# Attention stages two and three: score products issued ahead of the transposes, and one-pass float32r products for batches 4 to 7

## The reference, cut to what matters

```python
# first cross attention (stage "at2"): x_context has 77 tokens
q = layernorm((x_query @ Wq).reshape(B, Nq, H, D).transpose(0, 2, 1, 3), ln_g, ln_b) * SCALE
k = layernorm(k, ln_g, ln_b)
attn = jax.nn.softmax(jnp.einsum('bhqd,bhkd->bhqk', q, k), axis=-1)
out = jnp.einsum('bhqk,bhkd->bhqd', attn, v)
return out.transpose(0, 2, 1, 3).reshape(B, Nq, H * D) @ Wp + bp
# second cross attention (stage "at5"): the same with a mask
scores = jnp.einsum('bhqd,bhkd->bhqk', Q, K) / jnp.sqrt(jnp.float32(D_K))
attn_w = jax.nn.softmax(jnp.where(mask, -jnp.inf, scores), axis=-1)
```

## Time and profile before

| | |
|---|---|
| runs of the kernel before | median 405.69 us of 3 (404.98 to 406.9) |
| profiled execution | 410.61 us, span 408.8 us |
| mean granted clock of TensorE in it | 0.976 |
| busy of the span | PE 371.3 us (91%), DVE 285.3 (70%), ACT 223.5 (55%), POOL 142.3 (35%) |
| chain that ended last | PE 77%, DVE 12%, ACT 6%, issue 3% |
| `at2`, first `scores` to last `weigh` | 68.8 to 116.2 us |
| `at5`, first `scores` to last `weigh` | 264.5 to 308.2 us |

### The profile page before, as it was taken

One profiled execution on the slowest core, in us unless ns is written; L12 is line 12 of the kernel. 1 busy time (PEld: TensorE's weight loads), 2 busy tenths in 40 slices (PEclk: granted clock), 3 DMA queues, 4 the chain that ended last, 5 costly groups with the idle time before them and its releaser, 6 DMA issues.

```text
span 408.8 us, 10122 instructions
## 1 busy us (share of the span) xinstructions
PE 371.3 (91%) x4062; PEld 254.5 (62%) x4066; DVE 285.3 (70%) x729; ACT 223.5 (55%) x423; POOL 142.3 (35%) x130
## 2 busy tenths in 40 slices
PE   5989997798998999999999999789998999999990
PEld 2556675666775846566677777456774566666670
DVE  6767878447875785789899786676876544444456
ACT  2855568445568167899999981235454522222210
POOL 6929952571232150027889782100012000000002
PEclk9999999669999999999999999999999999999996
DMA  6420000000000000132232310360000000000001
GB/s 176 87 52 4 4 2 2 2 2 3 2 2 2 0 2 0 22 102 79 84 111 87 106 40 2 110 201 3 4 3 1 2 0 1 2 0 2 0 2 52
DMA packets 16883, 13.86 MB, mean 34 GB/s; under 512 B 6548, under 2 KB 14133, under 8 KB 16837
## 3 DMA queue, kind: packets, MB, share of 16 engines
q1 hardware_dynamic: 15538, 12.51, 10.5%
q10 hardware_dynamic: 1299, 0.71, 0.6%
HBM read 12.64 MB, written 0.57 MB: 32 GB/s over the span
## 4 chain that ended last, share of the span: by engine, by line
PE 77%; DVE 12%; ACT 6%; issue 3%; POOL 1%; POOLq 0%; DVEq 0%
PE PS L2005 10%; PE PS L2093 7%; PE PS L2097 7%; PE PS L2124 7%; PE PS L1581 6%; PE PS L1520 6%; PE PS L1601 5%; PE PS L1992 5%; PE PS L1560 5%; PE PS L1526 3%; PE PS L1650 2%; DVE mxp L1053 2%; PE PS L1515 2%; PE PS L1804 2%; DVE untransposed L1319 2%
## 5 line engine op out<-in xcount | busy, mean ns | idle before, releaser
L663 ACT ACTIVATE att<-PS 77x512 f32<-77x512 f32 (+1 forms) x96 | 51.7, 591 | 44.6 <-PE PS L1584 44.6
L1053 DVE TENSOR_REDUCE mxp<-PS 128x4 f32<-128x308 f32 (+1 forms) x96 | 48.1, 536 | 15.5 <-PE PS L1560 15.4
L910 ACT ACTIVATE kM<-PS 128x512 f32<-128x512 f32 x32 | 19.1, 597 | 55.4 <-PE PS L2093 55.4
L516 POOL TENSOR_TENSOR rstd<-ve,neg_half 128x1 f32<-128x1 f32 x24 | 14.2, 593 | 81.5 <-DVE ve L981 81.5
L510 POOL TENSOR_TENSOR rstd<-ve,neg_half 128x4 f32<-128x4 f32 x6 | 6.2, 1025 | 103.9 <-DVE ve L940 103.9
L1370 DVE TENSOR_TENSOR_SCAN big<-big,PS 128x768 f32<-128x768 f32 x22 | 38.3, 1747 | 5.2 <-PE PS L1992 4.8
L1459 DVE TENSOR_TENSOR big<-kM,PS 128x512 f32<-128x512 f32 x32 | 21.9, 687 | 27.3 <-PE PS L2097 26.0
L2093 PE MATMUL PS<-xT,V 128*128 128x512 f32 x64 | 33.0, 597 | 1.1 <-DVE xT L1447 0.8
L2097 PE MATMUL PS<-xT,V 128*128 128x512 f32 x64 | 32.7, 592 | 0.0
L2124 PEld LDWEIGHTS PS<-big 128*128 128x128 f32 x256 | 29.7, 192 | 3.4 <-issue 3.4
L2124 PE MATMUL PS<-big 128*128 128x128 f32 x256 | 29.7, 275 | 0.0
(11 more groups left out here) (367 smaller groups left out, 870.3 us busy)
## 6 DMA issues: line engine op xcount, KB each, us to landing
kM<-Cdram SPq DMA_DIRECT2D x6, 384.0 KB, 3.4
XH<-Cdram SPq DMA_DIRECT2D x5, 384.0 KB, 3.3
xT<-Cdram SPq DMA_DIRECT2D x5, 384.0 KB, 3.5
V<-in_L_ffn_Wg SPq DMA_DIRECT2D x1, 1024.0 KB, 5.6
V<-in_L_ffn_Wu SPq DMA_DIRECT2D x1, 1024.0 KB, 8.2
out_x<-X SPq DMA_DIRECT2D x2, 256.0 KB, 2.7
ctxN<-in_ctx ACTq DMA_DIRECT2D x1, 308.0 KB
X<-in_x ACTq DMA_DIRECT2D x1, 256.0 KB, 3.8
```

Source lines behind the costliest of these rows:

```text
L663: A_(PT[0:nk, i % 2, g], bank4(at.bank("exp", i, g), nk), ACT.Exp, scale=at.scale)\
L1053: V_.tensor_reduce(mxp[:, b % 3, g, 0:J], PS[:, at.bank("max", b, g), 0:J * nk].rearrange("p (j k) -> p j k", j=J), axis=AX.X, op=ALU.max) ...
```

## The change

Four things change in `at2` and `at5`; `at1` keeps its order.

1. PE issues `scores(i + 2)` ahead of `flips(i)` instead of behind it (with the order of the banks to match). ACT takes all four exponentials of a batch before its copy of `flipped`. DVE takes the four maxima right behind the copy of `outT`, and `residual`, the reciprocal and `normalise` come behind the remainders.
2. For batches 4 to 7 the products of `shifted` use new tiles `K4` and `Q4` in float32r. Each 32-row group now holds one head, 8 rows by 4 combinations of a high and a low part of key and query, so that one product sums high by high, low by high, high by low and low by low.
3. The parts are made by POOL (`split`: a copy that rounds to 12 bits, and a difference), for the late queries of `at2` by a second ACT copy and a DVE difference (`late_low`). SP stores each into a DRAM scratch in 4 transfers (`pack`), and POOL loads them back into `K4` and `Q4` (`unpack`). For `at2` one more ACT copy makes `key2_raw` from bank `k2.1`, behind the first of the four masked copies. For `at5` POOL makes the masked keys of the second half instead of DVE.
4. `keep_busy` gets 2 products ahead of `scores(0)` of `at2`, and 4 ahead of `scores(1)`. The load of the expert weights waits until the last packed part has been loaded.

```diff
+def slots(scores_first):
+    bursts = [("max", 0), ("flip", -1), ("max", 1)]
+    for i in range(B):
+        after = [("flip", i), ("max", i + 2)][::-1 if scores_first else 1]
+        bursts += [("exp", i)] + [(what, n) for what, n in after if n < B]
+    return [(what, i, g) for what, i in bursts for g in range(1 if what == "flip" else G)]
...
+        def pack(dst, high, low, n, order):
+            if n > 2:
+                sp.wait_ge(event(f"packed{n % 2}_stored"), 4 * 16 * ((n - 1) // 2))
+            rows = dst.rearrange("(h c d) n -> c h d n", c=4, d=HD)
+            for c, part in enumerate(order):
+                sp.dma_start(rows[c], high if part == "h" else low, allow_slow_non_contiguous=True)\
+                    .then_inc(event(f"packed{n % 2}_stored"), 16)
...
+        sp.wait_ge(event("split"), KEYS2_SPLIT)
+        pack_keys(k2_packed, key2_high, key2_low, 1)
+        for b in range(HB):
+            sp.wait_ge(at2.late, b + 1)
+            sp.wait_ge(event("late_low"), b + 1)
+            pack_queries(q2_packed[b], XH[:, b, :], XH[:, HB + b, :], 2 + b)
...
+        for b in range(HB):
+            sp.wait_ge(event("split"), QUERIES5_SPLIT[b])
+            pack_queries(q5_packed[b], sq[:, b, :], XH[:, b, :], 7 + b)
         sp.wait_ge(dring.full, dring.index["dl.1"] + 1)
+        sp.wait_ge(event("packed_loaded"), 16 * 10)
         sp.dma_start(Wg6, a["L1_ffn_Wg"].rearrange("e d n -> d e n")).then_inc(experts_loaded, 16)
...
+        def split(x, high, low, done):
+            P_.tensor_copy(high.bitcast(F32R), x).then_inc(event("split"), 1)
+            pool.wait_ge(event("split"), done - 1)
+            P_.tensor_tensor(out=low.bitcast(F32R), in0=x, in1=high, op=ALU.subtract).then_inc(event("split"), 1)
+        def unpack(dst, src, n):
+            pool.wait_ge(event(f"packed{n % 2}_stored"), 4 * 16 * ((n + 1) // 2))
+            if n > 1:
+                pool.wait_ge(event("packed_loaded"), 16 * (n - 1))
+            P_.dma_start(dst, src.rearrange("(g p) n -> p g n", g=G).bitcast(F32R),
+                         allow_slow_non_contiguous=True).then_inc(event("packed_loaded"), 16)
...
                 if 0 <= i < B:
-                    exponentials(i, (0, 1))
+                    exponentials(i, range(G) if at.scores_first else (0, 1))
...
+                if at.scores_first:
+                    if done:
+                        weighted_copy(at, n)
+                    if ahead:
+                        maximum(i + 2, 0)
+                        maximum(i + 2, 1)
...
+                        maximum(i + 2, 2)
+                        maximum(i + 2, 3)
+                        remainder(i + 2, 0)
+                    if left:
+                        apply(at, b)
+                    if ahead:
+                        remainder(i + 2, 1)
+                    if added:
+                        residual(at, r)
+                    if done:
+                        normalise(at, n, inverse(at, n))
+                    if added:
+                        statistics(at, r)
...
+                if at.packs(b):
+                    at.packed.wait_loaded(pe, b)
...
+                        if at.packs(b):
+                            keys, queries = at.packed.keys(g, j, b), at.packed.queries(g, j, b)
...
                 if 0 <= i - 1 < B:
                     weigh(i - 1)
+                if at.scores_first and i + 2 < B:
+                    scores(i + 2)
                 if i < B + 3:
                     flips(i)
...
         def queries_turned(n):
+            keep_busy(at2.bank("max", 0, 1), 2)
...
+        def first_half_scored():
+            pe.wait_ge(at1.residual_ready, B)
+            keep_busy(at2.bank("max", 1, 0), 4)
```

218 lines of the change are left out of this document (146 added, 72 removed).

## The result

The changed kernel takes 413.32 us (median of 4 executions, 410.77 to 415.28), the kernel before 406.26 beside it; the ratio is 1.015, with a 95% interval of 1.0095 to 1.0205. The forecast was 406.1, with a range up to 409.4. The profiled execution took 410.77, with a mean granted clock of 0.991; the other three had 0.979 to 0.983.

The account below looks back on a forecast made before the run. In `at5` PE was taken as full in a 5.15 us ring that includes DVE's first maximum. `at5` +0.1, `at2` 0.0 and small waits 0.3 gave +0.4 on the median: 406.1 us, range 402.6 to 409.4.

Parts of the forecast that it names:

- The new order: Scores right behind `weigh`, `normalise` last: +0.6 us in `at5`; +0.3, -0.3 in `at2`; -0.2 for step 0 of each stage.
- The ring through `normalise`: `weigh` of the next batch waits for DVE's `normalise`; this closed cycle was summed to 5.44 us in `at5`, 4.88 in `at2`.
- Float32r: Batches 4 to 7: four shifted products take 0.06 to 0.12 us instead of 0.23; counted as -0.3 us in each stage.
- steps 4 and 5: Steps of each stage with every ring member; there float32r's saving lies in PE's new wait and gives nothing.
- The key copy: ACT's fifth copy ahead of the copy of `xT` in `at2` delays late queries and `shifted(0)`: +0.5 us.
- The packed parts: Stores (3.6 us) and POOL's load in `at2` take 5.5 to 7.0 us plus POOL's issue, before `shifted(4)` at 7.8.
- The slack: Time left between batch 4's load in `at2` and its deadline at `shifted(4)`: 0.4 to 1.9 us.
- The rival: Loads come late, `shifted(4)` and later batches wait in `at2`, POOL holds back layer norm powers: +3, 409 us; chance 0.22.
- a half-clock stretch that the new gaps of PE bring: New gaps of PE make TensorE's clock fall to half, giving a slower result; chance 0.03.
- The clock rival: Timed executions also fall to half clock; added busy products keep `at2`'s first stretch at full clock: 403.4 us; chance 0.20.

Follow-up runs that it names:

- `at5_r_old_order`: Changed kernel without `at2`'s packed parts (float32 there) and with the order of before in `at5`, which keeps float32r: 402.6 us, ratio 0.9892 to the kernel before.
- `at2_old_at5_old_r`: Changed kernel with the order of before in both stages and float32r with packed parts in `at5` alone: 404.1 us, ratio 0.9953 to the kernel before.
- `at5_r`: Changed kernel without the packed parts, stores and loads of `at2`, whose batches 4 to 7 are float32 again: 405.2 us, ratio 0.9945 to the kernel before.
- `sp_loads`: Changed kernel, but SP issues the loads of `at2`'s packed parts, each behind its stores, instead of POOL: 412.2 us, ratio 1.0035 to the kernel before.
- `f32_traffic`: Changed kernel with float32 shifted products everywhere; parts still made, stored and loaded, but nobody waits for them: 411.9 us, ratio 1.0121 to the kernel before.
- `loads_in_time`: Changed kernel, but `at2`'s float32r products read queries from the packed keys, loaded in time; all transfers still run: 409.4 us, ratio 1.0044 to the kernel before.
- the shifted best kernel: Kernel with new order in `at2` only and float32r in `at5` only, its 8 starting busy products made as 64 of 64 columns: 409.8 us instead of 402.6.
- `at2_r`: Changed kernel with float32 and no packed parts in `at5`; `at2` keeps float32r, parts and transfers: 411.7 us, ratio 1.0104 to the kernel before.

## Why the prediction was wrong

**The new order** was sized nearly right: forecast +0.6 in `at5` and +0.3 less 0.3 and 0.2 in `at2`; measured 0.5 in `at5` (24.96 against 24.48), -0.8 in `at2` (`at5_r_old_order` against `at2_old_at5_old_r`; its full steps take 4.76, not 4.88), and no difference over all that the clock leaves visible. Beside float32r the order costs more in `at5`, 2.0 us over five batches (24.65 against 22.65), because it keeps float32r's gain from coming through. The ring through `normalise`, given as 5.44 us, shows in `at5_r` as 4.99, 4.99, 5.18, 5.65 and 5.32 from `weigh` to `weigh`, the last three with the residual and the waits for `oN`.

**Float32r**: forecast 0.06 to 0.12 us for four products beside the subtraction's 0.06; measured 0.12 for the two together, so the lower end. The prediction read from the passes of the Trainium skill ("FP8 and Floating Point Precision", TensorE Precision Notes) that such a group costs as the bfloat16 one, and the trace agrees: 0.06 us are left for it. That the gain would be hidden in steps 4 and 5 was right for this order: `at5_r` gains 0.3 us over five batches.

**The key copy** cost the 0.5 us given.

**The packed parts** are the step that failed: "The slack is 0.4 to 1.9 us." For batch 4 it was minus 1.5. The main term is the stores, forecast at 3.6 us: from the first issue to POOL's load 5.15 went by. SP needed 0.61 us for a store (2.45 for four, `sp_loads`) and not the 0.43 of the earlier trace rows, which show transfers of another kind, and a store of 64 KB landed in 2.8 us instead of 1.9. Here the sum had one value and no upper bound, although the trace of before has 64 KB transfers that took 3.5 to 5.0 us as well (`bp`, `Wo`, `bv`). The load was within its terms for batch 4, 3.52 us with POOL's issue against 2.3 to 3.8, but took 5.03 for batch 5 (94.31 to 99.34); POOL's issue took 0.78 us where I had 0.43 as a lower bound. And the deadline was 7.2 us instead of 7.8, since the steps of `at2` ahead of batch 4, which lack residual and apply, take 4.43 (80.03, 84.46, 88.89 for `weigh`) and not 4.7.

The rival had the mechanism and, with about 2 in 10, too small a chance, and its +3 us was too small a price as well. Its second half, POOL holding back the layer norm's powers, was named and not priced, and is 1.16 us of PE in `f32_traffic`. The Trainium skill ("SBUF — State Buffer", "SBUF: two separate sides") has it that some DVE instructions lock POOL out while it writes descriptors. No run here isolates that, and it was not needed for the miss: POOL's issues of queries took 0.78 to 0.79 us in `at2`, and what POOL waited for ahead of them was the stores.

The late loads are only a part of the loss. They are worth 2.8 us by `loads_in_time`, out of 5.7 at equal clock. By the traces the 5.7 are 2.1 net in `at2`, with the short half-clock stretch behind the wait and less what the new order gives, and 3.5 in `at5`, where the gaps are.

**What my cases hardly held** is what a wait does to the clock. "0.03 for a half-clock stretch that the new gaps of PE bring" was an afterthought. At a clock of 0.991 the changed kernel took 410.8 us (one execution) and the one before takes 405.1 at 0.99 or more: 5.7 us of loss. The other 1.4 us between the medians (7.1) go with lower clocks. The nine kernels that move parts in `at2` have median clocks of 0.964 to 0.985; of the ten others that I ran nine have 0.985 to 0.995 and one, the shifted best kernel, 0.978, and the kernel before has 0.984. Seven of the nine wait for a late load by 0.9 us or more. In six of these the clock falls in or just behind a wait of 1.3 to 2.9 us, to 0.50 to 0.67 over 4 us; in `at2_r`, with a longest wait of 2.0 us, it does not. In the two without such a wait, `f32_traffic` and `loads_in_time`, it is 1.00 from 88 to 120 us. So the waits are one way to the lower clocks, not a certain one, and how much of the loss they make by it was not isolated.

**The clock rival** (403.4) failed: the profiled execution was at full clock until the first late load, as it said, but the median of before was not at half clock in both stretches, and the waits brought new ones. Its opposite reading, mine, that the median had "little of these stretches", holds for 44 of 120 executions; the median one, 1.9 us slower than these, has by its time about one.

**The gaps in `at5`** were in no case, and they are the larger part of what the changed kernel loses at equal clock: 3.5 us by the length of the three `weigh`, and `weigh(1)` to `weigh(6)` took 2.5 us more than in `at5_r` with the same instructions on every engine there. Their cause stays open.

## What to carry to other kernels

Price a round trip through DRAM from transfers of the same shape and queue, issue by issue, and set it against the period that the changed kernel will have, not the old one; if it fits by the lower bounds only just, do not count on it. A load that waits for a store should not stand in an engine's list ahead of something that others wait for. And before believing a difference of one or two per cent, run the kernel with its instructions at another place: here a change that does nothing to the result moved one kernel by 7 us. When two traces differ in what is studied, compare their clock at the same place before giving the cause.

## What was not expected of the hardware

- One program, unchanged, has three levels of time (405.1, 407.0, 410.8 us) that go with its mean granted clock (0.99 and over, 0.98 to 0.99, under 0.98).
- PE can stand still for 0.5 to 1.3 us near the end of a run of products whose inputs are all there, with nothing that the profile shows it to wait for. Four kernels have it at the same three places; a fifth, with the same program of PE up to there, does not, after a half-clock stretch.
- 16 small products of one kind took 0.36, 0.51 and 0.77 us at full clock within one trace.
- Issuing a 64 KB store with rows scattered over partitions took SP 0.61 us, and a load of 256 KB took POOL 0.78 in `at2`.
